# Nine of sixteen gather batches copy into buffers, the vector engine adds them, and the last scatters are spaced

## The reference

```python
x = x + attn_a(layernorm(x))     # 16 heads of 8 channels, rotary, causal softmax
x = x + ffn(layernorm(x))        # layer 0 of the experts
x = x + attn_b(layernorm(x))     # one head of 128 channels, banded score, softmax
x = x + ffn(layernorm(x))        # layer 1 of the experts

# ffn: 64 experts of 128x128, each token takes 4 of them
sel_val, sel_idx = top_k(sigmoid(x @ expert_sel.T), 4)
out = sum over the 4 chosen e of (relu(x @ keys[e]) * sel_val[e]) @ values[e]
```

## Time and profile before

| what | value |
|---|---|
| median of 3 runs | 1334.67 us |
| lowest and highest of them | 1326.50 and 1334.81 us |
| the profiled execution | 1321.22 us |
| its span (first to last instruction) | 1319.5 us |
| mean granted TensorE clock | 0.806 |
| POOL, PE, DVE, ACT busy | 66, 63, 54, 42% of the span |

### The profile page before, as it was taken

One profiled execution on the slowest core, in us unless ns is written; L12 is line 12 of the kernel. 1 busy time (PEld: TensorE's weight loads), 2 busy tenths in 40 slices (PEclk: granted clock), 3 DMA queues, 4 the chain that ended last, 5 costly groups with the idle time before them and its releaser, 6 DMA issues.

```text
span 1319.5 us, 22434 instructions
## 1 busy us (share of the span) xinstructions
PE 832.7 (63%) x7290; PEld 611.6 (46%) x7290; DVE 711.2 (54%) x2037; ACT 559.9 (42%) x1505; POOL 876.3 (66%) x860
## 2 busy tenths in 40 slices
PE   1889887887787677978885254524767669900000
PEld 0534444443443267977874243423666669900000
DVE  2878988788783256645667475533555436500000
ACT  1177676766666434744543233121534336500000
POOL 6255577887675743478888878775304338888887
PEclk9699999899897779989987576656978779955555
DMA  6855553232712336888852222123435449943333
GB/s 179 287 204 190 179 172 100 74 103 87 219 56 81 112 92 173 245 196 204 180 100 39 44 45 35 44 44 102 123 105 144 120 126 271 245 67 44 44 43 48
DMA packets 235217, 163.80 MB, mean 124 GB/s; under 512 B 15968, under 2 KB 223840, under 8 KB 235104
## 3 DMA queue, kind: packets, MB, share of 16 engines
q1 hardware_dynamic: 185696, 112.00, 29.6%
q0 software_dynamic: 45056, 33.59, 14.5%
q10 hardware_dynamic: 4352, 16.78, 3.3%
HBM read 78.94 MB, written 83.36 MB: 123 GB/s over the span
## 4 chain that ended last, share of the span: by engine, by line
POOL 31%; PE 25%; issue 13%; DVE 12%; DMA 7%; ACT 5%; another core or an unknown queue 5%; SPq 1%; POOLq 0%; ACTq 0%; DVEq 0%
POOL x_res L1659 23%; DMA x_res<-result_rows,dest 6%; PE ps L630 4%; POOL sorted_rows L1647 4%; PE ps L729 4%; PE ps L738 3%; PE ps L589 3%; ACT arena L930 2%; PE ps L718 2%; SPq L452 1%; PE ps L677 1%; POOL arena L1691 1%; DVE row_max L1155 1%; PE ps L647 1%
## 5 line engine op out<-in xcount | busy, mean ns | idle before, releaser
L1659 POOL DMA_INDIRECT x_res<-result_rows,dest x256 | 397.9, 1554 | 100.2 <-issue 73.9
L930 ACT ACTIVATE arena<-ps 128x512 f32<-128x512 f32 x320 | 183.1, 599 | 83.4 <-PE ps L562 77.9
L1647 POOL DMA_INDIRECT sorted_rows<-v_aug,dest x128 | 124.5, 973 | 123.7 <-DVE dest L1342 55.5
L1647 POOL DMA_INDIRECT sorted_rows<-x_scaled,dest x128 | 127.4, 995 | 75.2 <-ACT x_scaled L896 39.3
L1354 DVE COPY arena<-ps 128x512 f32<-128x512 f32 x128 | 88.1, 689 | 145.6 <-PE ps L718 79.5
L729 PE MATMUL ps<-arena 128*128 128x128 f32 x1024 | 152.2, 297 | 21.3 <-DVE arena L1354 10.0
L738 PE MATMUL ps<-arena 128*128 x1024 | 145.3, 288 | 11.8 <-ACT arena L919 11.5
L919 ACT COPY arena<-ps 128x512 f32<-128x512 f32 x128 | 74.8, 584 | 182.5 <-PE ps L738 119.9
L729 PEld LDWEIGHTS ps<-arena 128*128 128x128 f32 x1024 | 138.4, 210 | 27.0 <-issue 14.4
L589 PE MATMUL ps<-arena 64*128 64x128 bf16 (+3 forms) x576 | 129.6, 304 | 32.0 <-DMA arena<-k_parts 17.9
L1155 DVE TENSOR_REDUCE row_max<-ps 128x1 f32<-128x512 f32 (+1 forms) x192 | 126.9, 681 | 35.0 <-PE ps L609 32.7
(11 more groups left out here) (202 smaller groups left out, 1507.3 us busy)
## 6 DMA issues: line engine op xcount, KB each, us to landing
arena<-sorted_rows SPq DMA_DIRECT2D x128, 256.0 KB
result_rows<-arena SPq DMA_DIRECT2D x128, 256.0 KB
sorted_rows<-arena ACTq DMA_DIRECT2D x16, 1024.0 KB, 4.6
arena<-q_parts SPq DMA_DIRECT2D x16, 512.0 KB
arena<-k_parts SPq DMA_DIRECT2D x16, 512.0 KB
q_parts<-parts SPq DMA_DIRECT2D x52, 128.0 KB, 2.7
k_parts<-parts SPq DMA_DIRECT2D x50, 128.0 KB, 2.9
x_res<-result_rows,dest POOLq DMA_INDIRECT x256
```

Of the source, the lines that this page charges most:

```text
L930: nc.scalar.activation(prob[:, grp % 2, pr % 2, PROB_AT[u]:PROB_AT[u] + T], ps[:, v % 2, :], ACT.Exp, scale=SCALE_A).then_inc(exp_done, 1)
L1647: g.indirect_dma_start(sorted_d[b // HALF][:, :], bass.IndirectOffsetOnAxis(dest[:, 16 * b + n:16 * b + n + 1], 0), scaled_rows(layer, b)[ ...
L1659: g.indirect_dma_start(x[:, TT * b + t, :], None, result_d[layer][b // HALF][:, :], bass.IndirectOffsetOnAxis(dest[:, at:at + 1], 0), comp ...
```

## The change

Nine of the sixteen gather batches, (0, 4) to (0, 7) and (1, 3) to (1, 7), become plain copies into a buffer; the other seven still add in the transfer. DVE adds the buffered rows to `x_res`, one instruction of 128 x 512 for each of the four choices, after the four transfers of that choice have landed. There are three buffers: `xs_a` and the two halves of `xs_b`. Layer 0 uses `xs_a` alone, so gather (0, 5) waits until DVE has done the four adds of (0, 4), and so on; layer 1 takes them in turn. For layer 0 the adds stand in `combined_stats`, in place of the bare wait; for layer 1 they stand behind DVE's last expert step, and SP sends a batch out when its adds are done. Besides, POOL clears `w_attn` (128 x 640 float32, dead by then) after each transfer of scatter (1, 5), (1, 6) and (1, 7).

```diff
+PLAIN = tuple((0, b) for b in range(4, B)) + tuple((1, b) for b in range(3, B))
+PACED_FROM = 5
+        gather_buffers = (xs_a, xs_b[:, 0], xs_b[:, 1])
+        def gather_buffer(layer, b):
+            return b % 3 if layer else 0
+        def last_reader(layer, b):
+            mine = PLAIN.index((layer, b))
+            earlier = [n for n in range(mine) if gather_buffer(*PLAIN[n]) == gather_buffer(layer, b)]
+            return TOPK * (earlier[-1] + 1) if earlier else 0
...
             for b in range(B):
-                for lane in landed:
-                    sp.wait_ge(lane, landed_count("gather", 1, b))
+                if (1, b) not in PLAIN:
+                    for lane in landed:
+                        sp.wait_ge(lane, landed_count("gather", 1, b))
+                else:
+                    sp.wait_ge(added, TOPK * (PLAIN.index((1, b)) + 1))
...
+            def add_rows(layer, b):
+                xb = x[:, TT * b:TT * b + TT, :]
+                for c in range(TOPK):
+                    for lane in landed:
+                        dve.wait_ge(lane, landed_count("gather", layer, b) - 16 * (TOPK - 1 - c))
+                    if c:
+                        dve.wait_ge(added, TOPK * PLAIN.index((layer, b)) + c)
+                    nc.vector.tensor_tensor(xb, xb, gathered_rows(layer, b)[:, TT * c:TT * c + TT, :], ALU.add).then_inc(added, 1)
...
             def combined_stats(b):
-                for lane in landed:
-                    dve.wait_ge(lane, landed_count("gather", 0, b))
+                if (0, b) in PLAIN:
+                    add_rows(0, b)
+                    dve.wait_ge(added, TOPK * (PLAIN.index((0, b)) + 1))
+                else:
+                    for lane in landed:
+                        dve.wait_ge(lane, landed_count("gather", 0, b))
...
             for s in range(STEPS):
                 expert_step(1, 1, s)
+            for b in range(B):
+                if (1, b) in PLAIN:
+                    add_rows(1, b)
...
+            def rest():
+                n = next(rests)
+                if n > 1:
+                    pool.wait_ge(rested, n - 1)
+                g.memset(w[:, :], 0.0).then_inc(rested, 1)
...
+                adding = (layer, b) not in PLAIN
+                if not adding and last_reader(layer, b):
+                    pool.wait_ge(added, last_reader(layer, b))
                 for c in range(TOPK):
                     for t in range(TT):
                         lane = next_lane()
                         at = 16 * b + TOPK * t + c
-                        g.indirect_dma_start(x[:, TT * b + t, :], None, result_d[layer][b // HALF][:, :],
-                                             bass.IndirectOffsetOnAxis(dest[:, at:at + 1], 0), compute_op=ALU.add).then_inc(lane, 16)
+                        rows, index = result_d[layer][b // HALF][:, :], bass.IndirectOffsetOnAxis(dest[:, at:at + 1], 0)
+                        if adding:
+                            g.indirect_dma_start(x[:, TT * b + t, :], None, rows, index, compute_op=ALU.add).then_inc(lane, 16)
+                        else:
+                            g.indirect_dma_start(gathered_rows(layer, b)[:, TT * c + t, :], None, rows, index).then_inc(lane, 16)
...
                     for n in range(TT * TOPK):
                         scatter(1, late, n)
+                        if late >= PACED_FROM:
+                            rest()
```

More of the change, by code:

```diff
@@ L376, in build @@
         scaled = sem("scaled")
+        rested = sem("rested")
+        added = sem("added")
         ln2 = sem("ln2")
@@ L398, in scaled_rows, with gathered_rows @@
             return xs_b[:, b % 2] if layer else xs_a
+        gather_buffers = (xs_a, xs_b[:, 0], xs_b[:, 1])
+        def gather_buffer(layer, b):
+            return b % 3 if layer else 0
+        def gathered_rows(layer, b):
+            return gather_buffers[gather_buffer(layer, b)]
+        def last_reader(layer, b):
+            mine = PLAIN.index((layer, b))
+            earlier = [n for n in range(mine) if gather_buffer(*PLAIN[n]) == gather_buffer(layer, b)]
+            return TOPK * (earlier[-1] + 1) if earlier else 0
         def evacuated(name, b):
@@ L1632, in _ @@
             g.tensor_tensor(maskswap, maskswap, upper, ALU.add).then_inc(swapped, 1)
-            transfers = count()
+            transfers, rests = count(), count(1)
+            def rest():
[3 more added lines that the diff above has]
+                g.memset(w[:, :], 0.0).then_inc(rested, 1)
             def next_lane():
```

## The result

The changed kernel takes 1294.95 us (median of 4 runs, 1293.4 to 1298.5); the kernel before, measured again beside it, takes 1331.18 us. The ratio is 0.9734 with a 95% interval of 0.9688 to 0.9779: 2.7% faster, 36 us. Forecast were 74 us. The sign was right, the size was half of it, and the time lies just above the range.

The account below looks back on a forecast made before the run. POOL's issue of indirect transfers was taken to bound the tail and the loop up to turn 6. Tail -44, loop -17, clears -6 and -7 make -74 us: 1334.7 - 74 = 1261 us, range 1230 to 1292.

Parts of the forecast that it names:

- The tail: Gathers (1, 3) to (1, 7): 80 plain gathers at the scatter's price, with adds mostly beside POOL's issue, give -44 us.
- the 2 us for DVE against POOL: Tail: DVE's 20 adds delay POOL's gathers by 2 us in all, between 0 and 14.
- the rival with 0.69 us for each add: Each add blocks POOL for its whole length: +12 us in the tail, little in the loop, 1273 us; chance 0.07.
- The prediction's own rule: Tail: a DVE add delays a gather only if it covers the moment 0.13 us after the gather's start.
- I take -7 together: Clears behind scatters (1, 5) and (1, 6): shrinking unassigned waits give -7 us, between 0 and -20.
- -6 for the stretch from scatter (1, 7) to the first gather: Clears behind scatter (1, 7): POOL ready after 31.5 us instead of 38.1, giving -6 us, between 0 and -7.
- The walk through POOL's order: Loop, gather (0, 4) to scatter (1, 3): four plain batches end that scatter at 877.4 instead of 894.3, -17 us.
- Turn 4: before, its stats began at 779.83; with the adds of turn 3 at 782.6: Loop: turn 4 starts only 2.8 us later, its adds end at 785.4, so gather (0, 6) doesn't wait.
- the first put it at 10 us a turn: Dense gathers hold up signals too: 10 us more in turns 3 to 6, loop gains nothing, 1285 us; chance 0.22.
- the second at 20 us a batch: Dense gathers in the loop cost DVE's path 4 x 20 = 80 us, net +30, 1365 us; chance 0.03.
- Its own signs of being wrong: Unassigned waits of 10 us or more at plain gathers, landings limiting the tail, or the (0, 5) gap at (0, 6), (0, 7).
- The stall of 25 us before gather (0, 5): Loop, turn 2 to 3: POOL stands 25 us waiting for DVE's adds of (0, 4), which need the one buffer.

Follow-up runs that it names:

- rests_only: The changed kernel with all sixteen gathers adding in the transfer, the clears behind scatters (1, 5) to (1, 7) kept: 1295.39 us against 1331.08 for the kernel before.
- rest_128: tail_rests with each clear behind a transfer cut from 640 to 128 columns, a transfer every 1.35 us: 1287.16 us.
- rest_256: tail_rests with each clear behind a transfer cut from 640 to 256 columns, a transfer every 1.46 us: 1274.59 us.
- tail_rests: The changed kernel with the four plain batches of layer 0 back to adding in the transfer; plain tail and clears kept: 1252.57 us.
- gathers_spaced: The changed kernel with a clear also behind each plain gather transfer of layer 0, scatters (1, 0) to (1, 4) left dense: 1253.14 us.
- three_spaced: all_spaced with more buffers in layer 0, so that no gather there waits for DVE's adds: 1270.48 us.
- all_spaced: The changed kernel with a clear behind every transfer of layer 1's scatters and of layer 0's plain gathers: 1273.73 us.

## Where the prediction was right and where it failed

**The tail: right, by its steps.** 80 plain gathers at the scatter's price (947 against 958 ns), no wait for landings (2.72 us for the last, against the 3.8 allowed), one add on the path, start of the tail not held by half (1, 1). -46.7 against -44; the 2 us for DVE against POOL didn't come. The rule of the Trainium skill that was weighed (SBUF — State Buffer, "Who interferes with whom") holds in its first half at the earlier trace rows. Its second half, in the form of the rival with 0.69 us for each add, is refuted for the tail: all 48 gathers into `v_aug` beside the adds take 941 to 957 ns. Here 19 of the 20 adds begin 0.03 to 0.30 us after a gather, as the prediction had it, so the case of the earlier trace rows, the DVE instruction first, doesn't occur; and the adds, coming second, take their 0.69 us, so a gather doesn't hold them up either. The prediction's own rule was too wide: it had any add that covers the moment 0.13 us into a gather delay it. The add at 1246.15 begins 0.03 us into its gather and covers that moment, and the gather takes 0.94 us; at the earlier trace rows the DVE instruction had begun first.

**The rests: right in kind, mis-sized.** The step says "I take -7 together" for scatters (1, 5) and (1, 6), and -6 for the stretch from scatter (1, 7) to the first gather. Measured with rests_only: `dest` (1, 5) to (1, 7) from 99.9 to 75.1 us (-25), and 38.1 to 28.4 us from scatter (1, 7) on (-10). The term rested on "some 8 and 3 us" as the cost of the waits, which no row showed; its range went to -20, and rest_128 and rest_256 show that the whole of it hangs on the spacing. A spaced scatter also came cheaper than 1.9 us, 1.78, since the 0.30 us of issue shrink to 0.17 behind a memset.

**The loop: wrong.** The walk through POOL's order kept the length of DVE's turns as before and added only the adds: 27 us for turn 3 to 4, 41 for the next, 38 for the last. The failing step is "Turn 4: before, its stats began at 779.83; with the adds of turn 3 at 782.6". They began at 821.62, 59.2 us after those of turn 3, and scatter (1, 3) ended at 923.6, 30 us later than before and not 17 earlier. Each turn took 53 to 61 us, since gather and scatter together are 40 us of dense issue in each, where before 30 of 50 us went to adding gathers every 1.85 us, beside which the others recover. The prediction named this mechanism, in two rivals with 0.25 of the chance together; the first put it at 10 us a turn and at a loop that gains nothing, the second at 20 us a batch. Measured are 42 us for four batches (tail_rests against the changed kernel), between the two. What it took for the likeliest was that dense issue hurts only as a scatter. Its own signs of being wrong came true: unassigned waits of over 10 us beside plain gathers, and the gap before (0, 5) back at (0, 6) and (0, 7). By medians the parts are -47 for the tail, -36 for the rests and +42 for the loop, -41 together against the measured -36. The same observation, and the earlier trace rows, fed one part of the sum and not the other.

**The stall of 25 us before gather (0, 5)** came as worked out. gathers_spaced keeps the wait in POOL's order and loses nothing against tail_rests, and three_spaced, without it, is no faster than all_spaced: the wait costs nothing by itself.

What stays open is the resource. What is shown is: it goes with the spacing of POOL's indirect transfers (scatters and plain gathers alike), with the number in flight not fully separated from it; it slows PE, DVE and ACT, and in the changed kernel PE's instructions without any wait too; it comes late in a dense stretch and outlasts it by some microseconds. Whether the way instructions reach the engines, the semaphores or the recording of the trace itself takes part can't be told, since every run here was made in the same way.

## What to carry to other kernels

Before an instruction is made cheaper, ask what the engine that issues it does with the time: a transfer every 1.26 us instead of every 1.85 us was a gain of 47 us where nothing else ran and a loss of 42 us beside work of many small instructions. If idle time "behind nothing" (issue, or an unassigned releaser) lines up with a dense stream on another engine, space that stream first and measure: 48 memsets that compute nothing gave 36 us. And one cause gets one price in the whole sum: a mechanism that is used to credit one part of a change has to be charged to every other part that feeds it.

## What the runs showed of the hardware that was not expected

- An indirect transfer that adds in float32 costs POOL 1542 ns, one that only copies 947 ns, with the same rows and indices.
- With indirect transfers every 1.26 us from POOL, weight loads and products of PE that wait for nothing start 1.4 us apart (37 times, almost all in the changed kernel's trace), and dependent small operations on DVE as well (837.67, 839.08, 840.50), there in the kernel before too. In all_spaced and three_spaced, at 1.78 us throughout, DVE has no such row.
- One stretch beside scatters takes 139 and 149 us with a transfer every 1.27 us (two traces), 146 at 1.35, 125 at 1.46 and 104 at 1.78; TensorE's mean granted clock in it goes from 0.74 and 0.80 up to 0.89.
- A DVE instruction with two SBUF inputs that had begun before a POOL transfer and still ran 0.3 us into it delayed it in 116 of 133 cases of the 13 traces; the transfer then ended 0.81 to 0.88 us after it (1.41 to 1.46 us for a gather that adds). One that began up to 0.11 us after the transfer delayed it by less than 0.1 us in all 213 cases.

```profile
784.12 1.22 DVE L1258 TENSOR_TENSOR one_hot<-iota_e,idxf 128x1024 bf16<-128x1024 f32 x1
784.20 1.99 POOL L1694 DMA_INDIRECT sorted_rows<-v_aug,dest  x1 [0.30 <-issue]
...
1246.12 0.94 POOL L1713 DMA_INDIRECT x_scaled<-result_rows,dest  x1 [0.30 <-issue]
1246.15 0.69 DVE L1392 TENSOR_TENSOR x_res<-x_res,v_aug 128x512 f32<-128x512 f32 x1 [4.27 <-DMA v_aug<-result_rows,dest]
```
